# A softmax taken by quads of heads: three engines share what ScalarE did alone, in four of six groups

## The reference, cut to what matters

```python
h = patchify(x) @ W.T + b;  h = concat([cls, h]) + pos          # 16 x 37 x 256
n = layernorm(h)
q, k, v = n @ Wq, n @ Wk, n @ Wv                                # 8 heads, 4 key and value heads, D = 128
q = q * cos + rotate_half(q) * sin                              # and k
attn = einsum('bhtd,bhsd->bhts', q, k) / sqrt(128)
attn = softmax(where(causal, -inf, attn), axis=-1)
h = h + einsum('bhts,bhsd->bhtd', attn, v) @ Wo
n = layernorm(h)
gate = top4(softmax(n @ router_w.T))                            # 16 routed experts, 2 shared ones
h = h + shared(n) + sum_e gate[e] * (gelu(n @ up[e].T) @ down[e].T)
```

## Time and profile before

| what | us |
|---|---|
| median of 3 executions (lowest, highest) | 155.99 (155.94, 156.2) |
| the profiled execution | 155.6 |
| its span, first to last instruction | 153.8 |
| outside the span in that execution | 1.8 |
| PE busy | 148.0 |
| DVE busy | 114.1 |
| ACT busy | 102.2 |
| POOL busy | 60.3 |

### The profile page before, as it was taken

The page is one execution under the profiler, slowest core; times in us unless marked ns, Lnnn a source line. Parts: engine busy times, 40 slices in busy tenths (PEclk is TensorE's granted clock), DMA queues, the critical chain, the costliest instruction groups (busy, mean ns, idle before and its releaser), DMA issues.

```text
span 153.8 us, 3280 instructions
## 1 busy us (share of the span) xinstructions
PE 148.0 (96%) x1089; PEld 138.7 (90%) x1089; DVE 114.1 (74%) x370; ACT 102.2 (66%) x290; POOL 60.3 (39%) x50
## 2 busy tenths in 40 slices
PE   6989999999999999999999999999999999999992
PEld 2878799998897898999889999999999999999991
DVE  0058768768897776586765758997989679959982
ACT  0306999786689999999586398847583744636700
POOL 0004999456736544403119400332517323354000
PEclk9999999999999999999999999999999999999999
DMA  4999910000000499600000000000000000000004
GB/s 146 341 382 365 402 35 0 0 0 9 0 0 0 142 428 419 242 2 6 0 0 4 0 0 0 0 6 0 2 0 4 0 2 0 0 4 0 4 2 158
DMA packets 5892, 11.95 MB, mean 78 GB/s; under 512 B 931, under 2 KB 3699, under 8 KB 5747
## 3 DMA queue, kind: packets, MB, share of 16 engines
q1 hardware_dynamic: 4434, 9.79, 17.2%
q10 hardware_dynamic: 1440, 1.95, 3.6%
HBM read 11.13 MB, written 0.61 MB: 76 GB/s over the span
## 4 chain that ended last, share of the span: by engine, by line
PE 77%; ACT 8%; DVE 6%; DMA 3%; ACTq 2%; issue 1%; POOL 1%; DVEq 0%
PE bank L1047 61%; PE bank L1164 5%; PE bank L1071 5%; DMA aux_sb<-aux_w 3%; ACT probs L505 3%; PE bank L1136 2%; PE bank L1188 1%; ACT swapped L494 1%; ACT swapped L493 1%; PE bank L1152 1%; PE bank L1091 1%; DVE qk L726 1%; ACTq L241 1%; ACTq L244 1%; POOL swapped L399 1%
## 5 line engine op out<-in xcount | busy, mean ns | idle before, releaser
L414 POOL TENSOR_TENSOR exp_lo<-ffn_sb,exp_hi 128x512 fp32r<-128x512 f32 x18 | 23.5, 1314 | 40.5 <-ACT exp_hi L527 40.5
L839 DVE SCALAR_TENSOR_TENSOR h<-bank,gate,h 128x256 f32<-128x256 f32 (+1 forms) x80 | 32.3, 473 | 1.1 <-PE bank L1047 0.9
L1047 PE MATMUL bank<-exp_hi,act_hi 128*128 128x256 f32 (+1 forms) x90 | 25.5, 284 | 0.1
L1047 PE MATMUL bank<-exp_lo,act_hi 128*128 128x256 f32 (+1 forms) x90 | 25.2, 280 | 0.0
L1047 PE MATMUL bank<-exp_hi,act_lo 128*128 128x256 f32 (+1 forms) x90 | 25.2, 280 | 0.0
L819 DVE TENSOR_TENSOR act_lo<-act,act_hi 128x256 fp32r<-128x256 f32 (+1 forms) x36 | 17.9, 522 | 5.8 <-ACT act_hi L539 5.6
L1047 PE MATMUL bank<-hnT_hi,exp_hi 128*128 128x256 f32 (+1 forms) x72 | 21.8, 303 | 0.0
L536 ACT ACTIVATE act<-bank 128x256 f32<-128x256 f32 (+1 forms) x36 | 15.3, 424 | 9.6 <-PE bank L1047 9.4
L1047 PE MATMUL bank<-hnT_hi,exp_lo 128*128 128x256 f32 (+1 forms) x72 | 21.5, 298 | 0.0
L1047 PE MATMUL bank<-hnT_lo,exp_hi 128*128 128x256 f32 (+1 forms) x72 | 21.4, 297 | 0.0
L399 POOL TENSOR_TENSOR swapped<-swapped,sin_sb 128x512 f32<-128x512 f32 (+1 forms) x12 | 17.3, 1449 | 9.9 <-ACT swapped L494 9.9
(11 more groups left out here) (92 smaller groups left out, 368.2 us busy)
## 6 DMA issues: line engine op xcount, KB each, us to landing
ffn_sb<-w_ffn SPq DMA_DIRECT2D x6, 768.0 KB, 7.9
wqkv_sb<-w_qkv SPq DMA_DIRECT2D x4, 512.0 KB, 9.1
wo_sb<-w_o SPq DMA_DIRECT2D x1, 1024.0 KB, 11.4
x_sb<-xT ACTq DMA_DIRECT2D x2, 384.0 KB, 6.5
out<-h SPq DMA_DIRECT2D x2, 256.0 KB, 2.2
x_sb<-xT ACTq DMA_DIRECT2D x3, 128.0 KB, 4.0
wp_sb<-wpT SPq DMA_DIRECT2D x3, 128.0 KB, 3.5
wp_sb<-wpT ACTq DMA_DIRECT2D x3, 128.0 KB, 4.3
```

What stands on the lines that cost most here:

```text
L414: nc.gpsimd.tensor_tensor(exp_lo[:, e % SPLIT_RING, :], ffn_sb[:, e, :], exp_hi[:, e % SPLIT_RING, :].bitcast(F32), ALU.subtract).then_inc ...
L839: last = nc.vector.scalar_tensor_tensor(h[r, i, :], y, gate[r, i, one], h[r, i, :], ALU.mult, ALU.add)
L1047: last = nc.tensor.matmul(ps, a, b, start=(n == 0 and m == 0), stop=(n == len(pairs) - 1 and m == 2 and not more))
```

## The change

For groups 2 to 5 (`g >= BY_QUAD`) the softmax of a quad goes another way. `less_max` stays. A new GpSimd step `above_least` subtracts the row's least from the whole quad in place, ScalarE takes one exponential over the quad without a bias and without sums, and VectorE's `inv_sum` adds up the rows with one `tensor_reduce` before its reciprocal. Groups 0 and 1 are as they were. Beside that, the written order of the calls is another one on all four engines, from the first layer norm to the last expert.

```diff
+BY_QUAD = 2
+        sc_above = sem("sc_above")
+        sc_sum = sem("sc_sum")
+            def above_least(g, c):                                   # POOL
+                pool.wait_ge(sc_less, 2 * g + c + 1)
+                nc.gpsimd.tensor_tensor(quad(probs, g, c), quad(probs, g, c), per_head(slow, g, c),
+                                        ALU.subtract).then_inc(sc_above, 1)
             def exps(g, c):                                          # ACT
+                if g >= BY_QUAD:
+                    act_e.wait_ge(sc_above, 2 * (g - BY_QUAD) + c + 1)
+                    nc.scalar.activation(quad(probs, g, c), quad(probs, g, c), ACT.Exp, scale=-1.0).then_inc(sc_exp, 1)
+                    return
             def inv_sum(g, c):                                       # DVE
                 dve.wait_ge(sc_exp, 2 * g + c + 1)
+                if g >= BY_QUAD:
+                    nc.vector.tensor_reduce(ssum[0:GN[g], g, QUAD * c:QUAD * c + QUAD], quad(probs, g, c),
+                                            AX_X, ALU.add).then_inc(sc_sum, 1)
+                    dve.wait_ge(sc_sum, 2 * (g - BY_QUAD) + c + 1)
                 nc.vector.reciprocal(sinv[...], ssum[...]).then_inc(sc_inv, 1)
```

More of the change, by code:

```diff
@@ L420, in _ @@
                 qkv_low(n)
-            for n in range(0, 12):
+            for n in range(0, 11):
                 sine(n)
             normalise(0, 0)
+            sine(11)
             normalise(0, 1)
             normalise(1, 0)
+            above_least(2, 0)
+            above_least(2, 1)
             normalise(1, 1)
@@ L638, in _ @@
             keep_turned(8)
-            gelu(1)
-            gelu(2)
             keep_turned(9)
-            for n in range(3, 6):
+            for n in range(1, 6):
                 gelu(n)
@@ L890, in _ @@
             cosine(4)
+            turned_low(4)
             rope_add(3)
@@ L959, in _ @@
             norm_stats(9)
-            zero_logits()
+            norm_apply(9)
             turned_low(8)
-            norm_apply(9)
             turned_low(9)
-            for n in range(0, 5):
+            act_low(0)
+            router_less_max()
+            for n in range(1, 6):
                 act_low(n)
-            router_less_max()
-            act_low(5)
             pick_top()
@@ L974, in _ @@
             add_expert(1, 1)
-            act_low(6)
-            act_low(7)
+            for n in range(6, 9):
+                act_low(n)
             add_expert(1, 2)
@@ L980, in _ @@
             add_expert(2, 2)
-            for n in range(8, 12):
-                act_low(n)
             add_expert(3, 0)
             add_expert(3, 1)
+            act_low(9)
+            act_low(10)
             add_expert(3, 2)
@@ L987, in _ @@
             add_expert(4, 1)
+            act_low(11)
             add_expert(4, 2)
             add_expert(5, 0)
-            for n in range(12, 16):
+            act_low(12)
+            add_expert(5, 1)
+            add_expert(5, 2)
+            for n in range(13, 17):
                 act_low(n)
-            add_expert(5, 1)
-            act_low(16)
-            add_expert(5, 2)
             add_expert(6, 0)
             add_expert(6, 1)
+            act_low(17)
+            act_low(18)
             add_expert(6, 2)
@@ L999, in _ @@
             add_expert(7, 1)
-            for n in range(17, 21):
-                act_low(n)
             add_expert(7, 2)
+            act_low(19)
             add_expert(8, 0)
@@ L1006, in _ @@
             add_expert(9, 0)
-            for n in range(21, 24):
+            add_expert(9, 1)
+            for n in range(20, 23):
                 act_low(n)
-            add_expert(9, 1)
             add_expert(9, 2)
+            for n in range(23, 26):
+                act_low(n)
             add_expert(10, 0)
@@ L1015, in _ @@
             add_expert(11, 1)
-            for n in range(24, 27):
-                act_low(n)
+            act_low(26)
             add_expert(11, 2)
@@ L1024, in _ @@
             add_expert(13, 0)
+            for n in range(29, 33):
+                act_low(n)
             add_expert(13, 1)
-            for n in range(29, 32):
-                act_low(n)
+            act_low(33)
+            act_low(34)
             add_expert(13, 2)
@@ L1030, in _ @@
             add_expert(14, 1)
-            for n in range(32, 36):
-                act_low(n)
+            act_low(35)
             add_expert(14, 2)
@@ L1252, in _ @@
             values(1)
+            turn_norm(4)
             project(5)
@@ L1350, in _ @@
             down(8, 0)
-            for n in range(18, 24):
-                up(n)
             down(8, 1)
```

243 lines of the change are left out of this document (127 added, 116 removed).

## The result

The changed kernel takes 158.18 us (median of 4 executions, 157.65 to 158.69) beside 156.09 (4 executions, 155.94 to 156.66): a ratio of 1.0127 [1.0084, 1.0169]. The forecast was 157.0, with a range up to 158.0: slower, as forecast, but by 1.5 to 2.1 us instead of 1.0. The first median lies 0.2 us beyond the range, the second inside it.

What follows compares the result with a forecast made beforehand. PE's own work was taken as the floor, busy 148.0 of 153.8 us, with only its waits winnable. Terms (a) to (h) summed to +1.0 us, giving 157.0 us; range 155.1 to 158.0.

Steps and rivals of the forecast that it cites:

- (a): First layer norm: norm_apply(2) now ahead of norm_stats(3) on DVE delays project(0); +0.2 us, between 0 and +0.4.
- (b): turn_probs(0,0), now directly behind values(5), waits for the last keep_v; +0.85 us.
- (c): attend(0,0): PE waits 0.5 us for ACT's exps(1,1) and keep_pT, as before; 0.
- (d): attend(1,0): its wait goes, -0.5 us; places near 61.6 and 68.6 to 70.3 go too, -0.55.
- (e): attend(4,0), attend(4,1), turn_norm(6) wait behind DVE's list, +1.2 us; old waits at attend(4,0) and two turn_norm go, -1.0.
- (f): project_out(4) waits for heads_low(5,1), with only route(0) left between attend(5,1) and it; +0.7 us.
- (g): Router: down(1,1) waits for the first add_expert 0.55 us instead of 0.3, as route(4) is no longer between; +0.25.
- (h): Experts: other places for high_parts and up blocks cover a wait near 127 us; -0.15 us, between -0.3 and +0.5.
- Faster by ACT's queue: Rival: ACT's queue was behind all attention waits, so its relief removes those of (c) and (e); 154.9 us, chance 0.22.
- POOL as the bound: Rival: POOL becomes attention's bound, its passes held up by 0.5 us each, units late; 158.3 us, chance 0.08.
- Not as said: Rival: the quad's single exponential costs as much as four, so ACT is late again; 157.8 us, chance 0.03.
- The rule of the Trainium skill: Two-input elementwise operations belong on VectorE, GpSimd taking about twice as long; above_least would be 1.23 us, the sum 0.6 larger.

Runs made afterwards that it cites:

- fix_fr: Changed kernel with attend(5,*) before project_out(3), heads copies of (5,1) before tile 7's, router and tile 8 order as before: 158.18 us, ratio 1.0141.
- after_no_sum: Changed kernel without VectorE's row sums (tensor_reduce of groups 2 to 5), reciprocal taken of another small tile: 157.43 us, 1.0096 to the kernel before.
- soft_only: Kernel before with the new softmax in groups 2 to 5, its above_least passes put into POOL's old list: 157.36 us, ratio 1.0079.
- before again: The kernel before, unchanged, measured again beside itself: 156.05 us beside 156.14, ratio 1.0000.
- quads_2_3: Kernel before with the new softmax in groups 2 and 3 only, normalise(2,1) and turn_probs(1,0) moved: 155.95 us, ratio 0.9998.
- after again: The changed kernel, unchanged, measured a second time: 157.64 us, ratio 1.0097 to the kernel before.

## Why the prediction was half right

The direction was right, and so was the reading that PE's few waits decide and that ACT's 7 us are not what they wait for. The waits that I had to find by going through the lists were partly others. By the prediction's letters, forecast and measured in the changed kernel's trace:

| step | forecast | measured | what it was |
|---|---|---|---|
| (a) first layer norm | +0.2 | 0.0 and +0.2 (two executions) | from the second `aux_parts` matmul to `project(0)` 5.85 us before, 5.86 and 6.15 after, of which 0.1 is a shorter first matmul; in the second, ACT waited 0.56 for the q, k and v weights, so it isn't shown to be the order's |
| (b) `turn_probs(0,0)` | +0.85 | +0.99 | the chain forecast; the last `keep_v` starts 0.07 later than PE lets it, and the handoff into PE is 0.14 |
| (c) `attend(0,0)` | 0 | -0.2 | |
| (d) `attend(1,0)` and two places | -1.05 | -0.6 | from the start of `turn_probs(0,0)` to that of `turn_probs(4,0)`, without `project_out(2)`, PE takes 20.95 us before and 20.17 after: -0.8 for (c) and (d) together |
| (e) old waits | -1.0 | -1.2 | with their restarts |
| (e) new waits | +1.2 | +0.84 | 0.67 and the restarts behind it; two gates, below |
| (f) `project_out(4)` | +0.7 | +0.93 | two gates, below |
| not in the list: `route(3)` | 0 | +0.40 | overlooked |
| (g) `down(1,1)` | +0.25 | +0.32 | |
| (h) experts | -0.15 | -0.2 | |
| sum | +1.0 | +1.3 to +1.5 | body +1.3 and +1.6 |

**The first step that failed is the one that isn't there, `route(3)`.** The prediction saw that `route(0)` had moved, and used that as a cover for (f); it did not ask what `route(0)` had covered in its old place. There its four matmuls (0.4 us) came first of sixteen in a row, and `route(3)`, the last four, started at 90.81, 0.10 after `keep_turned(8)` had ended: it had next to no room, and lost those 0.4 us. `route(3)` needs `keep_turned(8)`, which waits on ACT behind `gelu(0)` with its table load. ACT's timeline of the changed kernel; the copy of tile 8 is the first half of the last row, the one that `route(3)` starts after, at 92.61:

```profile
90.13 1.28 ACT L557 ACT_TABLE_LOAD   x1
...
91.97 0.31 ACT L491 ACTIVATE hnT_hi<-bank 128x160 fp32r<-128x160 f32 x1
92.15 0.82 ACT L498 ACTIVATE hnT<-bank 128x256 f32<-128x256 f32 x2
```

What removes this wait isn't shown: in `fix_fr` 0.38 of it stays although the two later `gelu` stand back in their old place. That the table load is its cause is not shown; it stands there in the kernel before as well.

**(f) was right in its chain, small in its handoffs, and had a second gate.** The chain is the one forecast: `attend(5,1)` ends at 84.19, `heads_high` runs from 84.23 to 84.65, `heads_low` from 84.68 to 85.15, PE starts at 85.31. The three handoffs are 0.04, 0.03 and 0.16 where the prediction had 0.1 for all, and `route(0)` covers 0.35 instead of 0.43: +0.93 and not +0.7. The same handoff into PE, from the end of the awaited instruction to the matmul, is 0.14 at (b) (`keep_v` ends at 53.73), where the prediction had 0.04; that is most of what (b) was too small by. Beside that, `project_out(4)` also waits for `keep_turned(7)`, since `turn_norm(7)` was moved to just before `attend(5,1)`. The prediction missed this one. It ends at 85.16. ACT's and DVE's timelines of the changed kernel:

```profile
84.23 0.42 ACT L539 ACTIVATE heads_hi<-bank 128x296 fp32r<-128x296 f32 x1
84.78 0.38 ACT L498 ACTIVATE hnT<-bank 128x256 f32<-128x256 f32 x1
```
```profile
84.68 0.47 DVE L794 TENSOR_TENSOR heads_lo<-bank,heads_hi 128x296 fp32r<-128x296 f32 x1
```

The two gates open within 0.02 us of each other. So the second costs nothing here, but it is where `fix_fr`, which mended the first and made the second later, lost more than it had won.

**(e) had one of two gates, and two waits too many.** It had `attend(4,0)` wait for `heads_low(3,0)`, behind the sums on DVE. One call earlier there is another gate that it missed: `turn_probs(5,0)` writes the bank that `keep_pT(4,0)` empties, and that copy stands on ACT behind `heads_high(3,1)`. ACT's and DVE's timelines of the changed kernel:

```profile
74.24 0.54 ACT L539 ACTIVATE heads_hi<-bank 128x444 fp32r<-128x444 f32 x1 [0.21 <-PE bank L1194]
74.68 0.71 ACT L535 ACTIVATE probsT<-bank 74x296 f32<-74x296 f32 x2
```
```profile
74.23 0.45 DVE L784 TENSOR_REDUCE ssum<-probs 74x4 f32<-74x296 f32 x1
74.71 0.17 DVE L787 RECIPROCAL sinv<-ssum 74x4 f32<-74x4 f32 x1
74.81 1.11 DVE L794 TENSOR_TENSOR heads_lo<-bank,heads_hi 128x444 fp32r<-128x444 f32 x2
```

The first copy ends at 75.08, PE starts `turn_probs(5,0)` at 75.23, 0.67 late. But the gate forecast is there too: `heads_low(3,0)` ends at 75.39, 3.07 us after PE is through `project_out(1)` (3.3 forecast), and `attend(4,0)` starts at 75.54, 0.05 later than the transposes let it. By these starts PE would have stood for 0.7 us there without the wait before them, close to the 0.8 of the prediction. Without the sums (`after_no_sum`) that 0.05 goes and the 0.67 stays, so taking out the sums opens one gate of two and wins nothing. What (e) had too much is the 0.1 before `attend(4,1)` and the 0.3 before `turn_norm(6)`: both come directly behind the matmuls before them. The prediction's main reason for slower, "chains of DVE and ACT handoffs, where DVE gets 4.3 us more", is right for the quads in the old order, where the sum makes 0.6% of 0.8%; in the new order the chain is there, but so is one without the sums.

**The rivals.** *Faster by ACT's queue*: (d) and the old waits of (e) went with the relief and the order together; with the relief alone (`soft_only`) the waits of 0.5 before `attend(1,0)` and `attend(4,0)` stay. The new waits of (e) came, and the new order's handoffs at (b) and (f) are not queue. *POOL as the bound*: without `above_least` the changed kernel is not faster; in the old order the pass costs 0.3%. *Not as said*: refuted by the 574 ns. *The rule of the Trainium skill* (GPSIMD Engine Reference, section Engine selection), by which the prediction estimated 1.23 us for the pass over 444 elements: the row has 0.926, so this case's trace doesn't bear out a factor of two; it is 1.5. What is left of the difference from +1.0 to +1.5: `route(3)` has 0.4; (b), (f) and (g), sized too small, and (d), sized too large as a gain, have 0.9 together; (c), (e) and (h) take back 0.8; (a) is between. That the lettered terms add up to the forecast (+0.9 to +1.1 measured) is partly luck, as their misses cancel. The further 0.5 us of the first measurement isn't explained.

## What to carry to other kernels

When a call is moved in a hand-written order, ask twice: what does it wait for in its new place, and what did it hide in its old one; and at each new wait list every gate, not the first that is late, because undoing one of two gates that open together gains nothing. Seven microseconds taken from an engine that is busy 97% of a stretch bought nothing here, as each unit's way from scores to product got longer and the added pass landed on an engine that carries a chain PE needs. Where that engine has no such chain (here groups 2 and 3) the added passes cost nothing, but they won nothing either. Compare small changes from a marker behind the start of the span, if the start varies from execution to execution.

## What the runs showed of the hardware

The start of the span isn't steady: the same first product got through 19, 16, 17, 14, 13 and 13 matmuls by 8.2 us in six executions (before, before again, `soft_only`, `quads_2_3`, after, after again). Behind the first of them they start 0.43 us apart until 4.53, 5.57, 4.77, 6.58, 7.09 and 6.88 us, and 0.22 apart from there, and at just these moments the trace's record of the granted clock begins, at full level; the 1.00 that the views print before it is no measurement. In all sixteen traces the same later matmul starts between 12.72 and 13.35, that is 0.6 us or 0.4% of the time. The pace isn't its only gate: in `fix_fr` the record begins at 4.36, and yet that matmul starts at 13.35, as PE waits 0.60 for `aux_parts`, on which DVE starts at 9.05 instead of 8.41, when the transfer has landed.

The pass over 444 elements on POOL took 926 ns on average in the changed kernel, with DVE's sums added, as `normalise` had in the trace before (928): no contention shows in it.
